# Value bias through spare contraction rows, and value blocks evacuated by ScalarE

## The chip, the cores and the metric

The kernel runs on one core of a Trainium2 chip. The metric is the device time of one launch in microseconds (us). The kernel before takes 1411.64 us (median of 3 runs, 1411.59 to 1412.21).

## The reference, cut to what matters

Input x has 16 batches of 512 tokens of width 128. Each batch is layer-normalised (xn), and the output is x plus an attention branch plus a feed-forward branch.

```python
q = einsum('bse,hde->bhsd', xn, Wq) + bq ; k = ... Wk + bk ; v = ... Wv + bv     # 16 heads of 64
scores = where(causal, -inf, q @ k.T / 8) ; att = softmax(scores) / 8
z = (att @ v).reshape(b, s, 1024) ; attention = z @ proj                          # 1024 x 128
base = xn @ W.T
lw = softmax(l2norm(xn @ Wp.T + bp) @ l2norm(sim) * exp(min(temp, c)))           # 4 experts
res = sum over experts of (lw if top1 else 0) * ((xn @ Wd.T) @ Wu.T)              # ranks 1, 2, 4, 8
out = x + attention + base + res
```

A row of softmax sums to 1, so the bias bv adds the same vector, bv / 8 carried through proj, to every token of the output. The attention weights are masked causally, and a softmax row still sums to 1 under the mask.

## The kernel before

**Units and steps.** A batch has 8 pairs of heads and 4 blocks of 128 queries, which makes 32 steps (`UNITS`). Step s handles pair s // 4 and block s % 4, whose scores are 128 x (128, 256, 384 or 512). Every engine walks the same list of steps, written out by hand in `step` functions, with semaphores between the engines. No planner reorders anything: the order of an engine's instructions is the order of the calls in its `step`.

**A unit's way.** TensorE (PE) writes the scores of both heads (L1046, L1049). VectorE (DVE) scales, masks and takes the maximum (`maximum`, L807). ScalarE (ACT) takes the exponentials with their sum (`exponentials`, L611). VectorE takes the reciprocal one step later (L796). GpSimd (POOL) multiplies by it (`normalise`, L534). TensorE transposes three steps after the scores (`LAG_T`, L1058), ScalarE copies head 0 out of PSUM (L622) and VectorE head 1 (L819). Once in four steps TensorE multiplies a pair by its values (`values`, L1082), nine steps after the pair began; ScalarE (L600) and VectorE (L825) split the result into a high and a low part, and `project` (L1094) multiplies that by proj. Four rotating buffers (`NROT`) hold the probabilities.

**Jobs.** `JOBS` lays other products over the steps, each in one of two PSUM banks (`jobp`, the step's parity): for each pair one q and one k product (L971), the router at step 5, the transposed xn of the next batch at step 25, the gated expert activations at step 26, and eight value blocks (128 tokens by 512 columns, L976) at steps 29, 30, 2, 6, 10, 14, 18 and 21. Steps 25 and 27 to 31 work ahead for the next batch. TensorE issues job s at the end of its step s, after `wait(pe, job_done[bank])` on the job before it in that bank. The other engines take up job s in their step s + 1. ScalarE does so early in the step, before its copy of the transposed probabilities (L622) and before its exponentials. VectorE does so late, after `maximum`, the reciprocal, L819 and L825. A value block is evacuated by VectorE alone in the kernel before: one `scalar_tensor_tensor` (L717) that multiplies by 1/8 and adds the bias, scaled once in the setup into `bv8` (L764). The bias reaches every partition by a broadcast DMA (L390).

**Other work around the change.** In step 21 VectorE gives the variances and GpSimd then normalises the next batch (`layernorm`, L490, L491, L496) before it goes on with the probabilities of unit 22. In step 22 TensorE transposes the finished sum into job bank 0 (L1119), and in step 23 VectorE adds the residual (`final`, L831). TensorE's k job of step 24 waits for that. In step 29 `lora` (L1108) adds the experts: one 96-row product of `wut` (up projections in three parts of 32 rows) with `gated_t` (the gated activations, same rows). SyncE issues all DMAs in order, among them the copies of q and k into `q_parts` and `k_twice` (L413, L417, L423), for which the next pair's scores wait.

**Setup.** GpSimd clears its tiles, makes the identity (L476) and the mask (L484) and normalises batch 0. TensorE transposes the weights. In batch 0, `rest` on TensorE (after step 0) transposes the small weights into `zp`, and `rest` on VectorE (after step 1) copies them out.

Of the kernel before, what the change touches and what calls it, by code (L numbers as in the profile page):

```python
# [34 lines left out]
F32 = mybir.dt.float32  # L35
F32R = mybir.dt.float32r
# [12 lines left out]
PROJ = 32  # L49
PARTS, PART = 3, NEXP * RMAX  # L50
NRD = PROJ + PART
LN_EPS = 1e-5
# [140 lines left out]
def build(nc, x, Wq, bq, Wk, bk, Wv, bv, proj, W, Wp, bp, sim, temp, Wd, Wu, out):  # L193
    with ExitStack() as ctx:
# [27 lines left out]
        up_parts = sb("up_parts", [P, PARTS, PART], F32R)  # L222
        wut = sb("wut", [PARTS * PART, E], F32R)
        bqk = sb("bqk", [P, 2 * NPAIR])
        bv8 = sb("bv8", [P, H * DH])
        bp_b = sb("bp_b", [P, PROJ])
# [46 lines left out]
        projs = pt[:, 1, 1, 0:2, :].rearrange("p a (c e) -> p (a c) e", e=E)  # L273
        bv_b = pt[:, 1, 1, 2:4, :].rearrange("p a b -> p (a b)")

# [14 lines left out]
        gated_parts = sb("gated_parts", [P, NBLK, PARTS, PART], F32R)  # L290
        gated_t = sb("gated_t", [PARTS * PART, S], F32R)

# [4 lines left out]
        proj_split = sem("proj_split")  # L297
        bv_loaded = sem("bv_loaded")
        sim_loaded = sem("sim_loaded")
        small_loaded = sem("small_loaded")  # L300
# [71 lines left out]
        def _(sp):  # L372
# [16 lines left out]
            load_weights(2, Wv)  # L389
            sp.dma_start(bv_b, bv.rearrange("h d -> (h d)").partition_broadcast(P)).then_inc(bv_loaded, 16)  # L390
            sp.wait_ge(zeroed, 8)
            sp.dma_start(small_in[:, 0, :], W).then_inc(small_loaded, 16)
            sp.dma_start(small_in[0:PROJ, 1, :], Wp).then_inc(small_loaded, 16)
# [69 lines left out]
        def _(pool):  # L463
# [6 lines left out]
            nc.gpsimd.memset(up_parts[:].bitcast(F32), 0.0).then_inc(zeroed, 1)  # L470
            nc.gpsimd.memset(small_in[:, 1:3, :], 0.0).then_inc(zeroed, 1)
            nc.gpsimd.memset(k_low[:].bitcast(F32), 0.0).then_inc(zeroed, 1)
            for e in range(NEXP):
                nc.gpsimd.memset(ramp[:, :, e:e + 1], float(NEXP - e)).then_inc(zeroed, 1)
            pool.wait_ge(zeroed, 8 + NEXP)
            nc.gpsimd.affine_select(out=ident[:], in_=ident[:], compare_op=ALU.not_equal, fill=1.0,  # L476
# [24 lines left out]
            layernorm(Counts(pool, -1))  # L501

            def pad_low_keys(c, s, setup=False):
# [4 lines left out]
                pool.wait_ge(zeroed, 8 + NEXP)  # L508
# [61 lines left out]
        def _(act):  # L570
# [7 lines left out]
            def job(c, s, back=0):  # L578
                kind, n = JOBS[s]
                bank = bank_of(s)  # L580
                if kind not in HI_KINDS:
                    return
                act.wait_ge(job_ready[bank], c.job(s, back))
                if kind == "xt":
                    nc.scalar.activation(xt_hi[:], jobp[bank][:], ACT.Copy)
                    nc.scalar.activation(by_parity(xq_hi[:]), evens_first(jobp[bank][:]), ACT.Copy)
                    nc.scalar.activation(xt[:], jobp[bank][:], ACT.Copy).then_inc(job_hi[bank], 1)
                elif kind == "k":
                    nc.scalar.activation(k_hi[:], jobp[bank][:], ACT.Identity,  # L589
                                         bias=bqk[:, NPAIR + n:NPAIR + n + 1]).then_inc(job_hi[bank], 1)  # L590
# [81 lines left out]
        def _(dve):  # L672
# [21 lines left out]
            def job(c, s, back=0):  # L694
                kind, n = JOBS[s]
                bank = bank_of(s)
                src = jobp[bank]
                if kind in HI_KINDS:

                    dve.wait_ge(job_hi[bank], c.hi(s, back))  # L700
                else:
                    dve.wait_ge(job_ready[bank], c.job(s, back))
# [8 lines left out]
                elif kind == "xt":  # L711
                    nc.vector.tensor_tensor(xt_lo[:], src[:], xt_hi[:].bitcast(F32), ALU.subtract)
                    done = nc.vector.tensor_tensor(by_parity(xq_lo[:]), evens_first(src[:]),  # L713
                                                   by_parity(xq_hi[:].bitcast(F32)), ALU.subtract)
                elif kind == "v":
                    cols = slice(S * (n // NBLK), S * (n // NBLK) + S)
# [39 lines left out]
            for s in AHEAD:  # L756
                job(before, s)
                if JOBS[s][0] == "xt":
                    weights(2)
                    dve.wait_ge(sim_loaded, 32)  # L760
                    nc.vector.tensor_scalar(temp_c[:], temp_b[:], CLAMP_MAX, None, ALU.min).then_inc(temp_ready, 1)
                if JOBS[s][0] == "k":
                    dve.wait_ge(bv_loaded, 16)
                    link(nc.vector.tensor_scalar(bv8[:], bv_b, INV_SCALE, None, ALU.mult))  # L764

# [11 lines left out]
            def rest():  # L777
# [5 lines left out]
                nc.vector.tensor_copy(wrd[:], zp[:, P:P + NRD]).then_inc(small_ready, 1)  # L783
                nc.vector.tensor_copy(wut[:], zp[0:PARTS * PART, 2 * P:3 * P]).then_inc(small_ready, 1)

# [152 lines left out]
            def batch(b, first, last):  # L938
                c = Counts(dve, b)
                for s in range(UNITS):  # L940
                    step(c, s, first, last)
                    if first and s == 1:
                        rest()

            batch(0, True, False)
# [9 lines left out]
        def _(pe):  # L955
# [192 lines left out]
            def batch(b, first, last):  # L1148
                c = Counts(pe, b)
                for s in range(UNITS):  # L1150
                    step(c, s, first, last)
                    if first and s == 0:
                        rest()

            batch(0, True, False)
# [30 lines left out]
```

## Time and profile before

| | |
|---|---|
| median of 3 runs | 1411.64 us |
| profiled execution | 1412.28 us |
| its span | 1410.0 us |
| granted TensorE clock, mean | 0.997 |
| busy: PE, PEld, DVE, ACT, POOL | 98%, 82%, 81%, 73%, 69% |

The profiled execution is 2.28 us longer than its span, which begins with the first instruction and ends with the last. PE is TensorE's matmul, PEld its weight load. A wait is the idle time of an engine in front of an instruction, put down to what released it. The ends of matmuls are modelled, so two neighbouring matmuls overlap in the rows, and distances between starts tell more than durations.

### The profile page before, as it was taken

What the parts mean: (1) busy time and instruction counts of PE and PEld (TensorE: products, weight loads), DVE (VectorE), ACT (ScalarE), POOL (GpSimd) and SP (SyncE); (2) the same over time, 40 slices, a digit from 0 to 9 for tenths busy, and PEclk for the clock granted to TensorE, in tenths of its full rate; (3) what the DMA queues carried; (4) which work ended last, traced back from release to release, by engine and by line L of the source; (5) the groups of instructions that cost most, each with busy time, mean ns of one, the idle gap of its engine ahead of it and who ended that gap; (6) DMA issues with size and microseconds to landing.
All of it is one profiled execution on the core that took longest, in us unless ns stands there. A gap on an engine that the chain in (4) does not pass through costs nothing. (4 is left out here: it accounts for less than half of the span.)

```text
span 1410.0 us, 34925 instructions
## 1 busy us (share of the span) xinstructions
PE 1378.1 (98%) x11036; PEld 1156.6 (82%) x11036; DVE 1141.5 (81%) x4134; ACT 1029.9 (73%) x3032; POOL 966.7 (69%) x1414
## 2 busy tenths in 40 slices
PE   6999999999999999999999999999999999999997
PEld 4778888788888888888888888888878888788886
DVE  6888878878788887977889788787878878888784
ACT  4777777777777776777777777777777777777774
POOL 5767767666676776767667676775776767677663
PEclk9999999999999999999999999999999999999999
DMA  6544444444454445444444544444444444444441
GB/s 154 117 102 103 116 112 94 110 116 102 106 116 115 94 106 123 95 115 100 113 109 109 121 95 106 113 113 106 103 110 112 98 117 110 113 100 112 106 98 46
DMA packets 113010, 151.91 MB, mean 108 GB/s; under 512 B 18175, under 2 KB 47166, under 8 KB 112830
## 3 DMA queue, kind: packets, MB, share of 16 engines
q1 hardware_dynamic: 112830, 149.68, 45.2%
q8 instruction: 92, 1.51, 0.5%
q14 instruction: 88, 0.72, 0.2%
HBM read 11.20 MB, written 4.19 MB: 11 GB/s over the span
## 5 line engine op out<-in xcount | busy, mean ns | idle before, releaser
L534 POOL TENSOR_TENSOR prob<-prob,rden 128x128 f32<-128x128 f32 (+3 forms) x1024 | 710.0, 720 | 383.4 <-DVE rden L796 381.1
L807 DVE CUSTOM_DVE_ANT_0 prob<-scores,mask 128x128 f32<-128x128 f32 (+3 forms) x1024 | 459.0, 484 | 233.1 <-issue 220.0
L611 ACT ACTIVATE prob<-prob,nmax 128x128 f32<-128x128 f32 (+3 forms) x1024 | 565.4, 556 | 69.1 <-DVE nmax L807 67.4
L1058 PE MATMUL ptp<-ident,prob 128*128 128x128 f32 x2560 | 370.5, 274 | 1.7 <-DVE pt L819 1.0
L622 ACT ACTIVATE pt<-ptp 128x128 f32<-128x128 f32 (+3 forms) x512 | 221.1, 432 | 170.3 <-PE ptp L1058 168.1
L1046 PE MATMUL scores<-k_twice,q_parts 128*128 128x128 f32 (+3 forms) x1024 | 328.4, 331 | 9.8 <-DMA k_twice<-k_hi 5.0
L1049 PE MATMUL scores<-k_low,q_parts 128*128 128x128 f32 (+3 forms) x1024 | 320.6, 323 | 0.0
L1058 PEld LDWEIGHTS ptp<-ident,prob 128*128 128x128 f32 x2560 | 295.4, 140 | 29.4 <-POOL prob L534 4.3
L1082 PE MATMUL zp<-pt,v_sb 128*64 128x64 f32 (+3 forms) x4096 | 307.7, 303 | 0.8 <-DVE z_lo L825 0.8
L1082 PEld LDWEIGHTS zp<-pt,v_sb 128*64 128x64 f32 x4096 | 221.5, 137 | 50.4 <-issue 22.3
L1046 PEld LDWEIGHTS scores<-k_twice,q_parts 128*128 128x128 f32 x1024 | 193.4, 189 | 67.8 <-issue 24.0
L819 DVE COPY pt<-ptp 128x128 f32<-128x128 f32 (+3 forms) x512 | 244.5, 478 | 4.3 <-PE ptp L1058 3.7
L1049 PEld LDWEIGHTS scores<-k_low,q_parts 128*128 128x128 f32 x1024 | 194.2, 190 | 19.2
L611 ACT ACTIVATION_READ_ACCUMULATOR prob<-prob,nmax 128x1 f32 x1024 | 197.1, 192 | 0.0
L513 POOL CAST k_low<-k_lo 64x512 fp32r<-64x512 f32 x256 | 155.9, 609 | 39.8 <-DVE k_lo L704 22.3
L600 ACT ACTIVATE z_hi<-zp 128x512 fp32r<-128x512 f32 x128 | 76.5, 598 | 120.5 <-PE zp L1082 119.4
L708 DVE SCALAR_TENSOR_TENSOR q_lo<-jobp,bqk,q_hi 128x512 fp32r<-128x512 f32 x128 | 94.7, 740 | 1.8 <-ACT q_hi L592 1.8
L704 DVE SCALAR_TENSOR_TENSOR k_lo<-jobp,bqk,k_hi 128x512 fp32r<-128x512 f32 x128 | 94.7, 740 | 0.0
L825 DVE TENSOR_TENSOR z_lo<-zp,z_hi 128x512 fp32r<-128x512 f32 x128 | 87.1, 681 | 3.2 <-ACT z_hi L600 3.2
L592 ACT ACTIVATE q_hi<-jobp,bqk 128x512 fp32r<-128x512 f32 x128 | 85.5, 668 | 4.6 <-PE jobp L971 4.6
L717 DVE SCALAR_TENSOR_TENSOR v_sb<-jobp,bv 128x512 f32<-128x512 f32 x128 | 87.0, 680 | 0.0
L589 ACT ACTIVATE k_hi<-jobp,bqk 128x512 fp32r<-128x512 f32 x128 | 86.3, 674 | 0.5 <-PE jobp L971 0.5
(141 smaller groups left out, 1689.7 us busy)
## 6 DMA issues: line engine op xcount, KB each, us to landing
k_twice<-k_hi SPq DMA_DIRECT2D x512, 128.0 KB, 2.4
q_parts<-q_hi SPq DMA_DIRECT2D x256, 128.0 KB, 2.4
q_parts<-q_lo SPq DMA_DIRECT2D x256, 128.0 KB, 2.4
xin<-in_L_attn_x_dram SPq DMA_DIRECT2D x16, 256.0 KB, 3.6
xres<-in_L_attn_x_dram SPq DMA_DIRECT2D x16, 256.0 KB, 3.1
out_dram<-osb SPq DMA_DIRECT2D x16, 256.0 KB, 2.5
pt<-in_L_attn_Wq_dram SPq DMA_DIRECT2D x1, 512.0 KB, 4.4
pt<-in_L_attn_Wk_dram SPq DMA_DIRECT2D x1, 512.0 KB, 4.8
```

The costliest lines, as they stand in the source:

```text
L513: nc.gpsimd.tensor_copy(k_low[own(h), h, n % 2, :], k_lo[own(h), :].bitcast(F32))\
L534: nc.gpsimd.tensor_tensor(part, part, scale, ALU.mult).then_inc(pn_ready, 1)
L611: nc.scalar.activation(part, part, ACT.Exp, bias=nmax[:, s % NROT, h:h + 1], scale=-1.0, accum_out=den[:, s % NROT, h:h + 1]).then_inc(p_r ...
L622: nc.scalar.activation(pt[:, p % 2, 0, 0:i + 1, P * i:P * i + P], src, ACT.Copy)\
L704: done = nc.vector.scalar_tensor_tensor(out=k_lo[:], in0=src[:], scalar=bqk[:, NPAIR + n:NPAIR + n + 1], in1=k_hi[:].bitcast(F32), op0=ALU ...
L708: done = nc.vector.scalar_tensor_tensor(out=q_lo[:, n % 2, :], in0=src[:], scalar=bqk[:, n:n + 1], in1=q_hi[:, n % 2, :].bitcast(F32), op0 ...
L807: nc.vector.tensor_tensor_reduce(out=prob[:, s % NROT, h, 0:cols], in0=scores[h][:, 0:cols], in1=mask[:, S - cols:S], scale=-INV_SCALE, sc ...
L819: nc.vector.tensor_copy(pt[:, p % 2, 1, 0:i + 1, P * i:P * i + P], src).then_inc(pt_ready[1], 1)
L1046: nc.tensor.matmul(scores[h][:, 0:width(s)], q_parts[:, h, p % 2, queries], k_twice[:, h, p % 2, 0:width(s)], start=True, stop=False)
L1049: nc.tensor.matmul(scores[h][:, 0:width(s)], q_parts[:, h, p % 2, queries], k_low[:, h, p % 2, 0:width(s)], start=False, stop=True).then_i ...
L1058: done = nc.tensor.transpose(ptp[h][:, P * j:P * j + P], prob[:, s % NROT, h, P * j:P * j + P], ident[:])
L1082: done = nc.tensor.matmul(zp[DH * odd:DH * odd + DH, z0 + P // 2 * j:z0 + S // 2], v_sb[:, j, col:col + DH], seen, start=j == NBLK - 1, st ...
```

## The change

Each value block is now evacuated by ScalarE as a copy scaled by 1/8, without a bias; VectorE does nothing for it. The bias enters through `lora`: `wut` and `gated_t` grow from 96 to 128 rows. The 32 added rows of `gated_t` hold zeros and ones that say which head a row of the kernel's reshaped output belongs to, 16 rows for the high and 16 for the low part. The added rows of `wut` hold bv / 8 carried through proj, one row for each head, in a high and a low part. They are made once: four small DMAs instead of the broadcast, three more memsets, three affine selects and one add on GpSimd, one more transpose in `rest`, eight matmuls after step 2 of batch 0 and two VectorE operations after step 3 of batch 0 (`value_bias`). The scaling of `bv8` goes from VectorE's setup, and a scaled copy `bvt` comes into its `rest`.

```diff
-            sp.dma_start(bv_b, bv.rearrange("h d -> (h d)").partition_broadcast(P)).then_inc(bv_loaded, 16)
             sp.wait_ge(zeroed, 8)
+            for part in range(2):
+                for odd in range(2):
+                    sp.dma_start(bv_rows[GATED + H * part:GATED + H * part + H, DH * odd:DH * odd + DH], bv)\
+                        .then_inc(bv_loaded, 16)
...
+            nc.gpsimd.memset(bv_rows, 0.0).then_inc(zeroed, 1)
             nc.gpsimd.memset(k_low[:].bitcast(F32), 0.0).then_inc(zeroed, 1)
+            nc.gpsimd.memset(token_heads, 1.0).then_inc(zeroed, 1)
+            nc.gpsimd.memset(late_rows[:], -1.0).then_inc(zeroed, 1)
...
+            rows_from(token_heads, 1, ROWS * GATED)
+            pool.wait_ge(heads_marked, 1)
+            rows_from(token_heads, -1, ROWS - 1 - ROWS * GATED)
+            nc.gpsimd.affine_select(out=late_rows[:], in_=late_rows[:], compare_op=ALU.is_ge, fill=0.0,
+                                    base=-(GATED + H), pattern=[[0, 1]], channel_multiplier=1).then_inc(heads_marked, 1)
+            pool.wait_ge(heads_marked, 2)
+            nc.gpsimd.tensor_tensor(gated_t[:], token_heads[:, 0:S], token_heads[:, S:2 * S], ALU.add)\
+                .then_inc(heads_marked, 1)
+            pool.wait_ge(heads_marked, 4)
...
# ScalarE, job
-                if kind not in HI_KINDS:
+                if kind not in HI_KINDS and kind != "v":
                     return
                 act.wait_ge(job_ready[bank], c.job(s, back))
+                if kind == "v":
+                    nc.scalar.activation(v_sb[:, n % NBLK, S * (n // NBLK):S * (n // NBLK) + S], jobp[bank][:], ACT.Copy,
+                                         scale=INV_SCALE).then_inc(job_done[bank], 1)
+                    return
...
# VectorE, job, setup and rest
+                if kind == "v":
+                    return
-                    done = nc.vector.scalar_tensor_tensor(
-                        out=v_sb[:, n % NBLK, cols], in0=src[:], scalar=INV_SCALE, in1=bv8[:, cols],
-                        op0=ALU.mult, op1=ALU.add)
-                    done = nc.vector.tensor_copy(gated_t[:], src[0:PARTS * PART, :])
+                    done = nc.vector.tensor_copy(gated_t[0:GATED, :], src[0:GATED, :])
-                    link(nc.vector.tensor_scalar(bv8[:], bv_b, INV_SCALE, None, ALU.mult))
+                nc.vector.tensor_scalar(bvt[:], zp[:, 3 * P:4 * P], INV_SCALE, None, ALU.mult).then_inc(small_ready, 1)
...
+            def value_bias():     # VectorE, after step 3 of batch 0
+                dve.wait_ge(bias_bank_ready, 1)
+                dve.wait_ge(heads_marked, 4)
+                link(nc.vector.tensor_copy(bias_hi[GATED:P, :], outp[GATED:P, 0:E]))
+                link(nc.vector.scalar_tensor_tensor(
+                    out=wut[GATED:P, :], in0=bias_hi[GATED:P, :].bitcast(F32), scalar=late_rows[GATED:P, 0:1],
+                    in1=outp[GATED:P, 0:E], op0=ALU.mult, op1=ALU.add))
...
# TensorE, rest
+                pe.wait_ge(bv_loaded, 64)
+                nc.tensor.transpose(zp[:, 3 * P:4 * P], bv_rows, ident[:])
+            def value_bias():     # TensorE, after step 2 of batch 0
+                pe.wait_ge(small_ready, 4)
+                pe.wait_ge(proj_loaded, 16)
+                for n in range(NPAIR):
+                    done = nc.tensor.matmul(outp[:, 0:E], bvt[:], projs[:, n, :], start=n == 0, stop=n == NPAIR - 1)
+                done.then_inc(bias_bank_ready, 1)
```

## Rows read from the trace of the kernel before

**Rows 1.** Waits, whole run: us in total, times, longest us

```profile
ACT pt L622 <- PE ptp L1058: 168.1, 211, 1.7
...
PEld jobp L971 <- DVE v_sb L717: 4.4, 20, 0.5
PEld ptp L1058 <- POOL prob L534: 4.3, 18, 0.7
```

**Rows 2.** Groups, ScalarE: a PSUM evacuation of a value block's size

```profile
L600 ACT ACTIVATE z_hi<-zp 128x512 fp32r<-128x512 f32 x128 | 76.5, 598 | 120.5 <-PE zp L1082 119.4
```

**Rows 3.** Timeline, TensorE, steps 0, 1, 4, 5: start, duration, operation

```profile
708.06 0.22 PE L1046 MATMUL scores<-k_twice,q_parts 128*128 128x128 f32 x1
...
709.85 0.27 PE L1046 MATMUL scores<-k_twice,q_parts 128*128 128x256 f32 x1
...
718.31 0.22 PE L1046 MATMUL scores<-k_twice,q_parts 128*128 128x128 f32 x1
...
719.86 0.28 PE L1046 MATMUL scores<-k_twice,q_parts 128*128 128x256 f32 x1
```

**Rows 4.** Timeline, VectorE and ScalarE, steps 31 and 0

```profile
794.03 0.68 DVE L717 SCALAR_TENSOR_TENSOR v_sb<-jobp,bv 128x512 f32<-128x512 f32 x1
...
792.47 0.28 ACT L622 ACTIVATE pt<-ptp 128x128 f32<-128x128 f32 x1 [0.37 <-PE ptp L1058]
```

**Rows 5.** Timeline, ScalarE, steps 3 and 22

```profile
717.00 0.28 ACT L622 ACTIVATE pt<-ptp 128x128 f32<-128x128 f32 x1 [0.37 <-PE ptp L1058]
...
767.25 0.60 ACT L622 ACTIVATE pt<-ptp 128x512 f32<-128x512 f32 x1 [1.42 <-PE ptp L1058]
```

**Rows 6.** Timeline, VectorE, steps 22 and 23

```profile
768.90 0.68 DVE L717 SCALAR_TENSOR_TENSOR v_sb<-jobp,bv 128x512 f32<-128x512 f32 x1
769.49 0.28 DVE L895 TENSOR_TENSOR gated<-dn,lg 128x128 f32<-128x128 f32 x1
...
771.41 0.68 DVE L831 TENSOR_TENSOR osb<-jobp,xres 128x512 f32<-128x512 f32 x1
```

**Rows 7.** Timeline, GpSimd, units 21 and 22 around the layer norm

```profile
767.92 1.19 POOL L534 TENSOR_TENSOR prob<-prob,rden 128x256 f32<-128x256 f32 x2 [0.84 <-DVE rden L796]
...
772.16 3.65 POOL L534 TENSOR_TENSOR prob<-prob,rden 128x384 f32<-128x384 f32 x4
```

**Rows 8.** Groups, GpSimd: one normalisation of 384 columns

```profile
L534 POOL TENSOR_TENSOR prob<-prob,rden 128x384 f32<-128x384 f32 x256 | 207.1, 830 | 187.8 <-DVE rden L796 187.8
```

**Rows 9.** Timeline, TensorE, k job of step 24; unit 22's second head in step 25

```profile
772.14 0.49 PE L971 MATMUL jobp<-xt_hi,w_hi 128*128 128x512 f32 x1
...
773.87 0.55 PE L1058 MATMUL ptp<-ident,prob 128*128 128x128 f32 x3
```

**Rows 10.** Timeline, GpSimd, setup

```profile
2.12 1.81 POOL L472 MEMSET k_low<- 128x2048 f32 x1
...
7.75 1.04 POOL L496 TENSOR_TENSOR xn<-xn,rstd 128x512 f32<-128x512 f32 x1
17.10 1.60 POOL L513 CAST k_low<-k_lo 64x512 fp32r<-64x512 f32 x2 [8.32 <-DVE k_lo L704]
```

**Rows 11.** Timeline, TensorE, setup and batch 0: steps 3, 5 and 8

```profile
9.62 1.06 PE L981 MATMUL jobp<-ident,xn 128*128 128x128 f32 x4
...
30.50 0.50 PE L1046 MATMUL scores<-k_twice,q_parts 128*128 128x512 f32 x1 [1.10 <-DVE nmax L807]
...
35.54 1.00 PE L986 MATMUL jobp<-wrd,xt 128*128 128x64 f32 x8
...
42.36 0.33 PE L1046 MATMUL scores<-k_twice,q_parts 128*128 128x128 f32 x1 [1.63 <-DMA k_twice<-k_hi]
```

**Rows 12.** Timeline, TensorE, batch 0: starts of steps 12 and 13

```profile
51.76 0.22 PE L1046 MATMUL scores<-k_twice,q_parts 128*128 128x128 f32 x1
...
53.91 0.39 PE L1046 MATMUL scores<-k_twice,q_parts 128*128 128x256 f32 x1
```

**Rows 13.** Windows: length, busy us and count of PE, PEld, DVE, ACT, POOL; granted clock; DMA

```profile
25.00:30.00 5.00, 4.19 (x14) 3.24 (x13) 3.54 (x15) 1.67 (x5) 1.98 (x4) 0.61 0.57 135
```

More of the change, by code:

```diff
@@ L50 @@
 PARTS, PART = 3, NEXP * RMAX
+GATED = PARTS * PART
 NRD = PROJ + PART
@@ L222, in build @@
         up_parts = sb("up_parts", [P, PARTS, PART], F32R)
-        wut = sb("wut", [PARTS * PART, E], F32R)
+        wut = sb("wut", [P, E], F32R)
+        bvt = sb("bvt", [P, P])
+        late_rows = sb("late_rows", [P, 1])
+        bias_hi = sb("bias_hi", [P, E], F32R)
         bqk = sb("bqk", [P, 2 * NPAIR])
-        bv8 = sb("bv8", [P, H * DH])
         bp_b = sb("bp_b", [P, PROJ])
@@ L273, in build @@
         projs = pt[:, 1, 1, 0:2, :].rearrange("p a (c e) -> p (a c) e", e=E)
-        bv_b = pt[:, 1, 1, 2:4, :].rearrange("p a b -> p (a b)")
+        bv_rows = pt[:, 1, 1, 2, 0:P]
+        token_heads = pt[:, 1, 0, 2:4, :].rearrange("p a b -> p (a b)")
         z_hi = sb("z_hi", [P, 2, NPAIR, OCT, ROWS], F32R)
@@ L290, in build @@
         gated_parts = sb("gated_parts", [P, NBLK, PARTS, PART], F32R)
-        gated_t = sb("gated_t", [PARTS * PART, S], F32R)
+        gated_t = sb("gated_t", [P, S], F32R)
         w_loaded = [sem(f"w_loaded{n}") for n in range(3)]
@@ L298, in build @@
         bv_loaded = sem("bv_loaded")
+        heads_marked = sem("heads_marked")
+        bias_bank_ready = sem("bias_bank_ready")
         sim_loaded = sem("sim_loaded")
@@ L471, in _ @@
             nc.gpsimd.memset(small_in[:, 1:3, :], 0.0).then_inc(zeroed, 1)
+            nc.gpsimd.memset(bv_rows, 0.0).then_inc(zeroed, 1)
             nc.gpsimd.memset(k_low[:].bitcast(F32), 0.0).then_inc(zeroed, 1)
+            nc.gpsimd.memset(token_heads, 1.0).then_inc(zeroed, 1)
+            nc.gpsimd.memset(late_rows[:], -1.0).then_inc(zeroed, 1)
             for e in range(NEXP):
                 nc.gpsimd.memset(ramp[:, :, e:e + 1], float(NEXP - e)).then_inc(zeroed, 1)
-            pool.wait_ge(zeroed, 8 + NEXP)
+            pool.wait_ge(zeroed, 11 + NEXP)
             nc.gpsimd.affine_select(out=ident[:], in_=ident[:], compare_op=ALU.not_equal, fill=1.0,
@@ L501, in _, with rows_from @@
             layernorm(Counts(pool, -1))
+            def rows_from(tile, step, base):
+                nc.gpsimd.affine_select(out=tile, in_=tile, compare_op=ALU.is_ge, fill=0.0, base=base,
+                                        pattern=[[step, tile.shape[1]]], channel_multiplier=-ROWS * step)\
+                    .then_inc(heads_marked, 1)
[6 more added lines that the diff above has]
+            nc.gpsimd.tensor_tensor(gated_t[:], token_heads[:, 0:S], token_heads[:, S:2 * S], ALU.add)\
+                .then_inc(heads_marked, 1)
+            pool.wait_ge(heads_marked, 4)
             def pad_low_keys(c, s, setup=False):
@@ L507, in pad_low_keys @@
                 scaled = 0 if setup else c.fixed(c.head(s, 1))
-                pool.wait_ge(zeroed, 8 + NEXP)
+                pool.wait_ge(zeroed, 11 + NEXP)
                 if not setup:
@@ L714, in job @@
                                                    by_parity(xq_hi[:].bitcast(F32)), ALU.subtract)
-                elif kind == "v":
-                    cols = slice(S * (n // NBLK), S * (n // NBLK) + S)
-                    done = nc.vector.scalar_tensor_tensor(
-                        out=v_sb[:, n % NBLK, cols], in0=src[:], scalar=INV_SCALE, in1=bv8[:, cols],
-                        op0=ALU.mult, op1=ALU.add)
                 elif kind == "router":
@@ L761, in _ @@
                     nc.vector.tensor_scalar(temp_c[:], temp_b[:], CLAMP_MAX, None, ALU.min).then_inc(temp_ready, 1)
-                if JOBS[s][0] == "k":
-                    dve.wait_ge(bv_loaded, 16)
-                    link(nc.vector.tensor_scalar(bv8[:], bv_b, INV_SCALE, None, ALU.mult))
             dve.wait_ge(small_loaded, 16 * n_small)
@@ L783, in rest @@
                 nc.vector.tensor_copy(wrd[:], zp[:, P:P + NRD]).then_inc(small_ready, 1)
-                nc.vector.tensor_copy(wut[:], zp[0:PARTS * PART, 2 * P:3 * P]).then_inc(small_ready, 1)
+                nc.vector.tensor_copy(wut[0:GATED, :], zp[0:GATED, 2 * P:3 * P]).then_inc(small_ready, 1)
+                nc.vector.tensor_scalar(bvt[:], zp[:, 3 * P:4 * P], INV_SCALE, None, ALU.mult).then_inc(small_ready, 1)
                 dve.wait_ge(simnorm_ready, 1)
@@ L943, in batch @@
                         rest()
+                    if first and s == 3:
+                        value_bias()
             batch(0, True, False)
@@ L1153, in batch @@
                         rest()
+                    if first and s == 2:
+                        value_bias()
             batch(0, True, False)
```

## The prediction

> **What bounds the kernel now.** The table of busy time comes first: TensorE is busy for 98% of the span, VectorE 81%, ScalarE 73%. The list of waits comes next, for what TensorE still waits for. Its weight loads stop 20 times for VectorE's copy of a value block, 4.4 us in all, and 18 times for GpSimd, 4.3 us; ScalarE stands 168.1 us waiting for TensorE's transposes [rows 1]. So TensorE's own order sets the end. The change takes no instruction from it, and can shorten the time only where TensorE stands. The timelines show where that is in a batch of some 88 us (1410 / 16): at the k jobs of steps 0 and 24, at the transposes of step 25 and around step 27. In between its starts follow one another at an even pace.
>
> **The steady part: what VectorE loses.** It sheds 8 operations of 0.68 us per batch [rows 4], 87 us in 16 batches. What this is worth is read at each place where TensorE waits.
>
> *Step 0.* The k job needs bank 0, which the value block of step 30 leaves when VectorE has copied it at 794.03 + 0.68 [rows 4]. Step 0 lasts 709.85 - 708.06 = 1.79 us; step 4, with the same instructions, 719.86 - 718.31 = 1.55 us [rows 3]. The difference, 0.24 us, is the wait and what it costs just after. ScalarE takes the same block in its step 31, before the copy in front of which it stands 0.37 us idle, at 792.47 [rows 4]. The value block's product is over by then, so ScalarE's copy ends near 792.8, two microseconds before TensorE needs the bank. The wait goes in 15 batches: 15 x 0.24 = 3.6 us. Nothing is late next: VectorE also loses the copy of the block of step 29, which stands in front of its maximum for unit 31, so that maxima, exponentials and the q copies of the pair come earlier as well.
>
> *Steps 23 to 25.* VectorE's value copy at 768.90 pushes what follows to 769.49, and with it `final`, which ends at 771.41 + 0.68 = 772.09 [rows 6]; TensorE's k job starts at 772.14, just behind [rows 9]. Without the copy, `final` ends some 0.59 us earlier (769.49 - 768.90), and so do the maxima of step 23. TensorE would arrive at step 25 that much sooner. But there it needs unit 22 from GpSimd, and GpSimd's order is fixed by something else: unit 21 at 767.92, as soon as VectorE's reciprocal of step 22 releases it, then the layer norm, then unit 22 from 772.16 [rows 7]. Two normalisations of 0.83 us [rows 8] end at 773.82, and TensorE's second head starts at 773.87 [rows 9]. That chain starts in front of the removed copy and has none of it in it. The 0.59 us are handed back in step 25: I count 0 here. The other end is the whole of it, 15 x 0.59 = 8.9 us.
>
> *Steps 27 and 28.* No value block lies between step 21 and this place, and the copies of steps 29 and 30 come after it: 0.
>
> **What ScalarE gains.** A copy of 128 x 512 out of PSUM takes it 598 ns [rows 2]; the scale is part of the instruction and there is no bias operand. 8 x 16 of them are 77 us more. In step 22 it lies in an idle 1.42 us; in steps 3, 7, 11, 15 and 19 the idle is only 0.37 us [rows 5], so 0.23 us stick out and push the exponentials of that step, the q and k copies and their DMAs. The units concerned are normalised far ahead of their transposes three steps later; the only place where TensorE regularly waits for GpSimd is step 25 (18 waits in 16 batches [rows 1]). I count 0; the other end is a rival below.
>
> The Trainium skill speaks against the move: "ScalarE: Activation LUTs", Rules for kernel authors, gives multiplications to VectorE and budgets about 0.3 us plus 0.83 ns per element on ScalarE, an estimated 0.73 us for this copy. The row has 0.598 us for the same shape against 0.68 us on VectorE, so the measurement decides against the rule here; by its price 0.36 us instead of 0.23 us would stick out.
>
> **`lora`.** 128 rows instead of 96 stream the same 512 columns. The nearest row is a 128-row product of 512 columns, 0.49 us [rows 9]. If rows cost time, a quarter of it would be the 32 new ones: at most 0.12 x 16 = 2.0 us, at least 0. I take 0, since the weight load is hidden beside the product in front of it and the stream of columns is unchanged.
>
> **Setup.** On GpSimd a memset of 2048 columns takes 1.81 us [rows 10], so 128 + 1024 + 1 more columns ahead of the identity are about 1.1 us. The layer norm ended at 8.79 (7.75 + 1.04 [rows 10]) and now ends near 9.9; TensorE took it up at 9.62 [rows 11]. Cost 0.3 us. The selects and the add that follow (some 4 us, scaled from the layer norm's 1.04 us for 512 columns) lie in the 8.32 us that GpSimd waits before 17.10 [rows 10]; 0, and if that cover were too short, the excess. The broadcast DMA goes and four short ones come on SyncE, ahead of loads that are needed only after step 0: 0. VectorE's scaling of `bv8` goes off no path, and the operation on `bvt` takes about 0.3 us in front of a maximum for which TensorE waits.
>
> **Batch 0.** One more transpose, 0.2 us. The eight matmuls: the router's four products are eight instructions within 1.00 us, about 0.1 us each at 64 columns [rows 11]; at 128 columns I take 0.11 us, and 16 x 0.11 = 1.8 us. TensorE stood 1.10 us before step 3 anyway [rows 11], so 0.7 us are new. Together 0.3 + 0.2 + 0.7 = 1.2 us, and 0.1 us for ScalarE's value copy in step 3. The wait of 1.63 us for k_twice before step 8 [rows 11] does not absorb them, since the q and k jobs of steps 3 and 4 that feed these DMAs move too. VectorE's two operations of about 0.3 us take the place of the value copy of step 2. Against this, batch 0 has no `project`, so TensorE is faster and runs into VectorE: step 12 lasts 53.91 - 51.76 = 2.15 us [rows 12] against 1.55 us later, 0.60 us of waits behind a value copy, and steps 16 and 20 are like it: 3 x 0.60 = 1.8 us that go. What goes at steps 23 and 24 is handed back in step 25 as above. Batch 0: 1.3 - 1.8 = -0.5 us.
>
> **The sum.** -3.6 - 0.5 = -4.1 us. The profiled execution took 1412.28 us (2.28 us more than its span) and would take 1408.2; the median of the runs lies 0.64 us lower, so 1407.5 us. The likeliest case has its own range: 1409.3 without the gain of batch 0, 1405.7 if setup and value bias cost only 0.2 us (1.1 less) and the later waits for k_twice shrink by 0.05 us in each batch.
>
> **Rivals.**
>
> *A. GpSimd does not hand the 0.59 us back.* Its chain from 767.92 would have to be shorter without VectorE working beside it. For it: GpSimd's wait at that place is released by VectorE. Against it: that release comes before the removed copy, and the distance from 772.16 to 773.82 is made of GpSimd's own durations. 1407.5 - 8.9 = 1398.6 us. 12%.
>
> *B. The start costs more.* TensorE's clock was granted at 0.61 between 25 and 30 us [rows 13], that is at half (1.2 GHz) for part of it, after an idle stretch. If the eight matmuls ran at half, 1.8 us more; if the gain of batch 0 fails too, another 1.8 us: 1411.1 us. 14%. "TensorE: Matmul & The Clock Gate" of the Trainium skill, Part 1, says that half clock is the default state and activity lifts it; by that rule the matmuls themselves would help to end it, and the row of 30 us and later would be the one to follow.
>
> *C. Slower: ScalarE becomes late.* Place: steps 3, 7, 11, 15 and 19. If TensorE stood for what sticks out, 5 x 0.23 x 16 = 18.4 us: 1425.9 us. It decides once the units behind have less than 0.23 us in hand before their transposes. For it: ScalarE goes from 73% to 79% and works in order, so a value copy blocks exponentials. Against it: the 18 waits for GpSimd, one per batch and all explained by the layer norm. 8%.
>
> *D. The change does not do what it says.* The wait at step 0 stays because TensorE finds another one there, the maximum of unit 31 or a DMA: 1407.5 + 3.6 = 1411.1 us. 6%.
>
> **How the numbers follow.** Forecast 60%, A 12%, B 14%, C 8%, D 6%. A run of this kernel can tell a difference of about 0.2%, 2.8 us, so faster means below 1408.8 us. Faster: 0.51 of the forecast's 0.60, and A's 0.12: 0.63. Same: the remaining 0.09, B and D: 0.29. Slower: C, 0.08. The range reaches from 1401.0, which holds a partial A, to 1412.5, which holds B and D with a us to spare; all of A and C, 20%, may lie outside.
>
> **What would show it.** Right: no wait of the k job for v_sb; step 0 lasts 1.55 us; `final` ends about 3.6 us after GpSimd starts on unit 21 instead of 4.17 (772.09 - 767.92), while unit 22's second head is transposed 5.95 us after GpSimd starts on unit 21 (773.87 - 767.92) as before; step 8 of batch 0 starts 1 to 1.5 us later and step 21 about 0.5 us sooner than in the trace of before. Wrong: step 25 no longer waits for GpSimd (A), TensorE waits for ScalarE's pt or for GpSimd in other steps (C), or a step 0 of 1.79 us (D).

## The result, and the profile after

The changed kernel takes 1407.54 us (median of 7 runs, 1405.42 to 1408.1), the kernel before 1412.21 us on the same chip (median of 7, 1411.08 to 1414.11). The ratio is 0.9965, with a 95% interval of 0.9953 to 0.9976. The forecast was 1407.5 us.

The profiled execution took 1408.1 us (span 1406.4, mean granted clock 0.997), against 1412.28 us (span 1410.0). The page after, its busy times:

```profile
PE 1371.4 (98%) x11053; PEld 1161.0 (83%) x11053; DVE 1093.6 (78%) x4008; ACT 1085.1 (77%) x3160; POOL 970.6 (69%) x1421
```

VectorE went from 81% to 78% and ScalarE from 73% to 77%. These are averages, and say nothing yet about the time. The list of waits (whole run: us in total, times, longest) answers [rows 1]:

```profile
ACT pt L654 <- PE ptp L1106: 102.0, 116, 1.6
...
ACT v_sb L613 <- PE jobp L1014: 13.2, 32, 1.1
...
PE ptp L1106 <- DVE pt L855: 7.2, 16, 0.8
...
PEld jobp L1009 <- DVE osb L867: 5.0, 15, 0.3
...
PEld ptp L1106 <- POOL prob L562: 4.4, 18, 0.7
```

TensorE no longer waits for v_sb. ScalarE lost 66 us of its idle time in front of L654 (168.1 in [rows 1]), which is where most of the 75 us of new copies went. The 18 waits for GpSimd are as before (15 of them in step 25, one for each batch but the last, and three in the tail of the last batch; the prediction put all 18 down to the layer norm), and so are the 15 for `final` (L867; before 5.0 us for L831). New are 16 waits of TensorE for VectorE's copy of transposed probabilities (L855), 7.2 us in all; in the kernel before that row has 1.0 us in 2 waits.

**Step 0.** TensorE's timeline (start, duration), steps 0 and 1, beside [rows 3]:

```profile
705.62 0.22 PE L1094 MATMUL scores<-k_twice,q_parts 128*128 128x128 f32 x1
...
707.16 0.28 PE L1094 MATMUL scores<-k_twice,q_parts 128*128 128x256 f32 x1
```

707.16 - 705.62 = 1.54 us; batches 1 to 15 have 1.55 to the rounding. It was 1.79. Batch 0 is another case, below.

**Steps 22 to 24.** First VectorE beside [rows 6], then GpSimd beside [rows 7], then TensorE beside [rows 9]:

```profile
765.92 0.68 DVE L861 TENSOR_TENSOR z_lo<-zp,z_hi 128x512 fp32r<-128x512 f32 x1
766.52 0.35 DVE L931 TENSOR_TENSOR gated<-dn,lg 128x128 f32<-128x128 f32 x1
...
768.02 0.89 DVE L937 CAST gated_parts<-gated 128x256 fp32r<-128x256 f32 x1
768.83 0.15 DVE L832 RECIPROCAL rden<-den 128x2 f32<-128x2 f32 x1
768.91 0.26 DVE L855 COPY pt<-ptp 128x128 f32<-128x128 f32 x1
769.09 0.67 DVE L867 TENSOR_TENSOR osb<-jobp,xres 128x512 f32<-128x512 f32 x1
```

```profile
765.54 1.18 POOL L562 TENSOR_TENSOR prob<-prob,rden 128x256 f32<-128x256 f32 x2 [0.89 <-DVE rden L832]
766.68 1.06 POOL L502 TENSOR_TENSOR rstd<-var_eps,power 128x4 f32<-128x4 f32 x1
767.72 1.04 POOL L503 TENSOR_TENSOR xn<-xin,meanvar 128x512 f32<-128x512 f32 x1
768.84 1.04 POOL L508 TENSOR_TENSOR xn<-xn,rstd 128x512 f32<-128x512 f32 x1
769.84 4.37 POOL L562 TENSOR_TENSOR prob<-prob,rden 128x384 f32<-128x384 f32 x6
```

```profile
768.49 0.41 PE L1106 MATMUL ptp<-ident,prob 128*128 128x128 f32 x2
769.31 0.41 PE L1106 MATMUL ptp<-ident,prob 128*128 128x128 f32 x2 [0.42 <-DVE pt L855]
769.82 0.50 PE L1009 MATMUL jobp<-xt_hi,w_hi 128*128 128x512 f32 x1
```

The value copy is gone: L931 follows 0.60 us behind the start of L861, where it used to follow 1.19 us behind (769.49 - 768.30). But `final` ends at 769.09 + 0.67 = 769.76, which is 4.22 us after GpSimd starts on unit 21 (765.54). Before it was 4.17. The 0.59 us are already lost inside VectorE, before TensorE can see them. One row shows where: the cast L937 takes 0.89 us. Before, the same instruction (L901) in the same place took 0.32 us:

```profile
770.91 0.32 DVE L901 CAST gated_parts<-gated 128x256 fp32r<-128x256 f32 x1
```

Both casts end 0.15 us after GpSimd's subtraction `xn<-xin,meanvar` ends: before 771.23 against 770.04 + 1.04 = 771.08 (L491), after 768.91 against 767.72 + 1.04 = 768.76 (L503). The cast came earlier by the whole removed copy, and waited until the same instruction of GpSimd was over. TensorE then stands in step 24 in front of L1106 and in front of the k job.

**Balance of the span.** From the starts of the batches: batch 1 starts 0.19 us later, batches 1 to 14 together 3.18 us shorter (14 times 0.24 is 3.36), and the last batch with the tail 0.67 us shorter. The sum is 3.66 us, the difference of the spans (1410.03 and 1406.37). An undisturbed batch went from 85.72 to 85.79 us down to 85.60. That is 0.12 to 0.19 us, the 0.24 us of step 0 less 0.06 in steps 23 to 25 (2.69 + 2.41 + 4.15 before, 2.62 + 2.54 + 4.15 now). The rest of the 3.18 us is that five of the 14 batches of before lasted over 86 us, four of them through a k_twice transfer that came late before step 4 and one (batch 2) through longer steps 16 and 24, and only one does now. The medians differ by 4.67 us, more than the spans, because the time outside the span fell as well: it is 1.70 to 1.92 us in the seven runs of the changed kernel and 2.28 us in the profiled execution of the kernel before. No term of the forecast had these 0.4 us.

### The profile page after: what moved, and what is told of

Same layout as the page of the kernel before. It is cut to its first block, busy times and chain, and to the rows that moved or that the text cites. A ratio compares the mean times of both kernels' runs of the same rounds, so it can differ in the third digit from the quotient of the medians.

```text
span 1406.4 us, 34974 instructions
## 1 busy us (share of the span) xinstructions
PE 1371.4 (98%) x11053; PEld 1161.0 (83%) x11053; DVE 1093.6 (78%) x4008; ACT 1085.1 (77%) x3160; POOL 970.6 (69%) x1421
## 4 chain that ended last, share of the span: by engine, by line
PE 52%; DVE 3%; issue 1%; ACT 1%; SPq 0%; DMA 0%; DVEq 0%
PE zp L1130 12%; PE ptp L1106 11%; PE jobp L1009 7%; PE scores L1094 7%; PE scores L1097 6%; PE jobp L1014 4%; PE outp L1142 3%; DVE prob L843 1%; PE jobp L1024 1%; DVE osb L867 0%; DVE gated_parts L937 0%; DVE xq_lo L747 0%; PE jobp L1019 0%; PE jobp L1167 0%; PE outp L1156 0%
## 5 line engine op out<-in xcount | busy, mean ns | idle before, releaser
L843 DVE CUSTOM_DVE_ANT_0 prob<-scores,mask 128x128 f32<-128x128 f32 (+3 forms) x1024 | 461.0, 486 | 276.1 <-issue 253.3
L1106 PE MATMUL ptp<-ident,prob 128*128 128x128 f32 x2560 | 372.1, 274 | 8.0 <-DVE pt L855 7.2
L1106 PEld LDWEIGHTS ptp<-ident,prob 128*128 128x128 f32 x2560 | 295.4, 141 | 37.5 <-issue 11.1
L654 ACT ACTIVATE pt<-ptp 128x128 f32<-128x128 f32 (+3 forms) x512 | 221.4, 432 | 104.0 <-PE ptp L1106 102.0
L855 DVE COPY pt<-ptp 128x128 f32<-128x128 f32 (+3 forms) x512 | 246.0, 480 | 4.3 <-PE ptp L1106 3.7
L861 DVE TENSOR_TENSOR z_lo<-zp,z_hi 128x512 fp32r<-128x512 f32 x128 | 87.1, 680 | 3.2 <-ACT z_hi L632 3.2
L613 ACT ACTIVATE v_sb<-jobp 128x512 f32<-128x512 f32 x128 | 75.0, 586 | 13.3 <-PE jobp L1014 13.2
```

The lines of the kernel that those rows point to most:

```text
L654: nc.scalar.activation(pt[:, p % 2, 0, 0:i + 1, P * i:P * i + P], src, ACT.Copy)\
L843: nc.vector.tensor_tensor_reduce(out=prob[:, s % NROT, h, 0:cols], in0=scores[h][:, 0:cols], in1=mask[:, S - cols:S], scale=-INV_SCALE, sc ...
L855: nc.vector.tensor_copy(pt[:, p % 2, 1, 0:i + 1, P * i:P * i + P], src).then_inc(pt_ready[1], 1)
L1106: done = nc.tensor.transpose(ptp[h][:, P * j:P * j + P], prob[:, s % NROT, h, P * j:P * j + P], ident[:])
```

## The experiments

Each kernel was timed beside the kernel before (1412.6 us in both sets), with 11 runs each, but 6 of the kernel without the value bias and 4 of the changed kernel with the layer norm split. Two theories stand at first. **Pinned:** GpSimd's layer norm holds both `final` (through the cast) and unit 22, so only step 0 gains. **Rival:** something that the change added (the start, ScalarE's copies) eats a gain that steps 23 to 25 would have had.

**No value bias.** It leaves the value bias out of the output, so that the price of the start shows.

```diff
-                nc.tensor.matmul(outp[:], wut[:], gated_t[:], start=False, stop=False, skip_group_check=True)
+                nc.tensor.matmul(outp[:], wut[0:GATED, :], gated_t[0:GATED, :], start=False, stop=False, skip_group_check=True)
...
-                    if first and s == 2:
-                        value_bias()
```

Its DMAs, memsets, selects, add, transpose and `bvt` go as well.

> The changed kernel without everything that makes the bias (four small DMAs, three memsets, the selects and the add on GpSimd, the transpose, the eight matmuls, the VectorE operations; lora with 96 rows), so bv is left out of the output. ScalarE still evacuates the value blocks. The theory that the start pays for the bias (1.0 us at step 8 of batch 0 in the trace of after): step 8 of batch 0 starts at 42.3 instead of 43.36 us, and the time is 1406.5, 1.0 us below the changed kernel. Rival, that the waits of batch 0 absorb the bias work: step 21 of batch 0 starts at 73.8 as before and the time is 1407.5.

1407.69 us (1405.88 to 1409.6), ratio 0.9968 [0.9957, 0.998]. In the trace step 8 of batch 0 starts at 42.30 instead of 43.36 us and batch 1 at 105.15 instead of 106.16: the bias costs 1.0 us, once, inside the span (the granted clock between 25 and 30 us is alike in the two traces, 0.55 and 0.59). The time is not 1.0 us lower, against the theory: outside the span these runs spend 2.08 to 2.17 us, some 0.3 us more than the changed kernel, and the runs do not resolve the rest. The steps of the steady part are the same, so the 128-row `lora` costs nothing that can be seen.

**Copies back on VectorE.** The bias stays in the spare rows, the value blocks go back to VectorE as scaled copies.

```diff
-                if kind == "v":
-                    return
...
+                elif kind == "v":
+                    done = nc.vector.tensor_scalar(v_sb[:, n % NBLK, S * (n // NBLK):S * (n // NBLK) + S], src[:],
+                                                   INV_SCALE, None, ALU.mult)
```

> The changed kernel with the value blocks evacuated by VectorE again, as a scaled copy without the bias operand; the bias stays in the spare rows. The theory that the gain is the k job's wait at step 0 and nothing of the bias path: a copy of about 0.68 us on VectorE brings back steps 0 of 1.79 us (15 x 0.24 = 3.6 us) and the waits of batch 0, with the price of the start on top: 1412 to 1413 us. Rival, that one operand less in VectorE's evacuation (or the bias path) already gave the gain: 1407.5 to 1409 us.

1412.26 us (1411.07 to 1414.17), ratio 1.0002 [0.9994, 1.0011]. Step 0 is 1.78 us again. So, within the 1.2 us that the interval leaves, the whole gain comes from the engine that copies, not from where the bias enters.

**Cast behind `final`.** Of the changed kernel: the cast that waits for GpSimd is issued later in step 23.

```diff
-                    router(c, 2 * s)
+                    if s != STEP_FINAL:
+                        router(c, 2 * s)
...
+                if s == STEP_FINAL:
+                    router(c, 2 * s)
                 router(c, 2 * s + 1)
```

> The changed kernel with one VectorE instruction moved within step 23: the cast of gated_parts, which ran 0.89 us instead of 0.32 us beside GpSimd's layer norm, is issued after final instead of ahead of the reciprocal. Theory A, that the cast waits for GpSimd's instruction to end and that unit 22's normalisation on GpSimd holds the same 0.59 us a second time: final ends 0.8 us sooner, the k job of step 24 no longer waits for it, the second head of unit 22 is still transposed 5.95 us after GpSimd starts on unit 21 or only as much earlier as the reciprocal of unit 22 moves, and the time stays within 2 us of 1407.5. Theory B, that the cast alone held the gain back: step 24 loses its 0.6 us and step 25 does not win them, 15 x 0.6 = 9 us less, 1398.5 us. In both the cast takes about 0.3 us plus whatever is left of GpSimd's instruction at its new place.

1414.21 us (1412.54 to 1417.71), ratio 1.0011 [1.0001, 1.0021]: slower than either theory had it. VectorE's timeline, then two rows of GpSimd's:

```profile
769.24 0.68 DVE L867 TENSOR_TENSOR osb<-jobp,xres 128x512 f32<-128x512 f32 x1
769.84 1.15 DVE L937 CAST gated_parts<-gated 128x256 fp32r<-128x256 f32 x1
771.02 0.80 DVE L941 TENSOR_TENSOR gated_parts<-gated,gated_parts 128x128 fp32r<-128x128 f32 x1
```

```profile
769.80 1.04 POOL L508 TENSOR_TENSOR xn<-xn,rstd 128x512 f32<-128x512 f32 x1
770.80 4.42 POOL L562 TENSOR_TENSOR prob<-prob,rden 128x384 f32<-128x384 f32 x6
```

`final` did come earlier: 769.92, which is 3.42 us after unit 21 begins at 766.50. But the cast now met the next instruction of the layer norm, L508, from its start, and again ended 0.15 us after it (770.99 and 770.84). L941, with two inputs in SBUF, then met the first normalisation. The maxima of step 24 came late behind both, and TensorE stood 1.14 us before step 25; an undisturbed batch takes 86.02 us, 0.4 us more than in the changed kernel. Delaying an instruction by some tenths only changes which GpSimd instruction it waits for.

This trace also warns of something else. Up to step 22 its batch 0 has the instructions of the changed kernel, and yet step 8 begins at 40.61 us instead of 43.36 and batch 1 at 103.62 instead of 106.16. The granted clock is 1.00 between 20 and 30 us here, and 0.72 and 0.59 in the two halves of that stretch in the changed kernel. So a difference of a microsecond or two in batch 0 between two single traces is not by itself the price of an edit.

**Layer norm split.** Of the changed kernel: GpSimd takes only the root in step 21 and does the subtraction and the multiplication after unit 22, so VectorE and TensorE no longer meet them there.

```diff
-            def layernorm(c):
+            def root(c):
...
+            def layernorm(c):
...
                     if s == STEP_VAR and not last:
+                        root(c)
+                    if s == STEP_VAR + 1 and not last:
                         layernorm(c)
```

`root` keeps the power (L502 of the changed kernel), `layernorm` the two others (L503, L508).

> The changed kernel with GpSimd's layer norm split: the root stays in step 21, the subtraction and the multiplication come after unit 22's normalisation instead of before it. Both things that pin steps 23 to 25 go: the cast finds GpSimd idle (0.29 us instead of 0.89), unit 22 is normalised as soon as its reciprocal is there. Theory A expects the waits for pt in step 24 and for GpSimd in step 25 gone (0.59 and 0.19 us) and the wait for final at 0 to 0.34 us: 0.7 to 1.1 us in each of 15 batches, 1391 to 1397 us. Rival, that TensorE then waits for unit 23, which GpSimd normalises later (3.06 and 2.50 us in hand now), or for the late xn in step 25: 1405 us or more.

1398.7 us (1396.03 to 1399.73), ratio 0.9902 [0.9886, 0.9917]: the fastest kernel of the study, 0.6% below the changed one, and 1.7 us above what theory A expected. VectorE, GpSimd and TensorE at the same place:

```profile
764.09 0.28 DVE L941 CAST gated_parts<-gated 128x256 fp32r<-128x256 f32 x1
764.29 0.15 DVE L836 RECIPROCAL rden<-den 128x2 f32<-128x2 f32 x1
764.37 0.26 DVE L859 COPY pt<-ptp 128x128 f32<-128x128 f32 x1
764.56 0.67 DVE L871 TENSOR_TENSOR osb<-jobp,xres 128x512 f32<-128x512 f32 x1
```

```profile
761.61 1.18 POOL L564 TENSOR_TENSOR prob<-prob,rden 128x256 f32<-128x256 f32 x2 [0.88 <-DVE rden L836]
762.76 1.06 POOL L501 TENSOR_TENSOR rstd<-var_eps,power 128x4 f32<-128x4 f32 x1
764.52 1.66 POOL L564 TENSOR_TENSOR prob<-prob,rden 128x384 f32<-128x384 f32 x2 [0.71 <-DVE rden L836]
766.15 1.04 POOL L504 TENSOR_TENSOR xn<-xin,meanvar 128x512 f32<-128x512 f32 x1
```

```profile
764.56 0.63 PE L1110 MATMUL ptp<-ident,prob 128*128 128x128 f32 x4
765.28 0.50 PE L1013 MATMUL jobp<-xt_hi,w_hi 128*128 128x512 f32 x1
...
766.57 0.82 PE L1110 MATMUL ptp<-ident,prob 128*128 128x128 f32 x6
```

With GpSimd idle the cast takes 0.28 us. `final` ends at 765.23, 3.62 us after unit 21 starts. The transposes of step 24 run without a break, and so do those of step 25. Step 24 lasts 1.94 us (2.54 in the changed kernel), step 25 3.96 (4.15), and a batch 84.83 us instead of 85.6. Of TensorE's waits around here only 0.34 us for `final` is left. These 0.78 us per batch are what was expected (0.7 to 1.1). What is missing lies in batch 0, where TensorE's clock was at its lower level, 1.2 GHz, twice. The windows below have length, busy us and count of PE, PEld, DVE, ACT, POOL, then clock, DMA share, GB/s. Between 25 and 30 us the clock is 0.50, and the first 1.5 us of the sixteen bias matmuls fall into it (each of the eight calls is two instructions in the trace): they take 2.67 us instead of 1.96. Step 8 still begins at 43.23 us, 0.13 sooner than in the changed kernel. The larger loss follows: TensorE stands 1.71 us for k_twice before step 8, the clock falls soon after (0.50 in a window from 43.77 to 47.18 us), and steps 8 to 11 take 11.02 us instead of 9.43. In the changed kernel the wait at that place is 1.58 us and the clock stays at 1.00. Batch 1 starts 0.77 us later for all this.

```profile
25.00:30.00 5.00, 4.79 (x18) 4.19 (x17) 4.47 (x20) 1.52 (x5) 1.99 (x4) 0.50 0.55 132
...
45.00:50.00 5.00, 5.00 (x45) 4.05 (x43) 3.06 (x9) 2.69 (x10) 4.59 (x8) 0.78 0.62 144
```

```profile
28.61 2.67 PE L1085 MATMUL outp<-pt,bvt 128*128 128x128 f32 x16
```

**No cast.** It leaves the cast out (a four-column memset keeps its semaphore), so the experts' high parts are stale. The question: if the cast alone is removed and the layer norm stays, is there a gain?

```diff
-                    nc.vector.tensor_copy(gated_parts[:, :, 0:PARTS:2, :],
-                                          gated[:].unsqueeze(2).to_broadcast([P, NBLK, 2, PART])).then_inc(r_chain, 1)
+                    nc.vector.memset(scratch[:], 0.0).then_inc(r_chain, 1)
```

> The changed kernel without the cast of gated_parts (a memset of 4 columns stands in its place, so the experts' high parts are stale in the output). VectorE then meets no port held by GpSimd ahead of final; GpSimd's order is untouched. Theory A, that unit 22's place behind the layer norm on GpSimd pins step 25 by itself: final ends about 3.6 us after GpSimd starts on unit 21 (4.22 in the changed kernel), step 24 shrinks from 2.54 to about 2.0 us, and step 25 grows by as much, so the second head of unit 22 is still transposed 5.95 us after that start: 1407.5 us within 1. Theory B, that the cast's wait alone held the gain: step 25 keeps its 4.15 us, 15 x 0.55 = 8 us less, 1399 us.

1410.08 us (1407.99 to 1412.58), ratio 0.9983 [0.9974, 0.9991]. No gain, though the cast is gone and `final` ends 3.42 us after unit 21 starts. Steps 24 and 25 last 2.19 and 4.49 us, in sum 6.68; with the cast 2.54 and 4.15, in sum 6.69. The 0.35 us won in step 24 return in step 25, where TensorE still waits for unit 22 and also for a maximum that stands behind the next VectorE operation, L941, which now meets GpSimd in place of the cast. Of the two waits the one for unit 22 ends last: its second head starts 6.00 us after GpSimd starts on unit 21, as with the cast (6.01). The rows are VectorE's, GpSimd's and TensorE's:

```profile
770.63 0.68 DVE L868 TENSOR_TENSOR osb<-jobp,xres 128x512 f32<-128x512 f32 x1
771.23 1.14 DVE L941 TENSOR_TENSOR gated_parts<-gated,gated_parts 128x128 fp32r<-128x128 f32 x1
```

```profile
771.18 1.04 POOL L509 TENSOR_TENSOR xn<-xn,rstd 128x512 f32<-128x512 f32 x1
```

```profile
772.63 0.39 PE L1094 MATMUL scores<-k_twice,q_parts 128*128 128x256 f32 x1 [0.30 <-DVE nmax L844]
...
773.89 0.55 PE L1106 MATMUL ptp<-ident,prob 128*128 128x128 f32 x3 [0.19 <-POOL prob L563]
```

L941 ends at 772.37, 0.15 us after L509 (772.22). A batch lasts 85.77 us, 0.17 more than in the changed kernel: the rest of its steps are up to 0.03 us longer each, for a reason that was not found, and 15 times that is the 2.5 us between the two medians, which neither theory had.

**The kernel before with the layer norm split.** The same edit as above, applied to the kernel before.

> The kernel before with GpSimd's layer norm split in the same way, value copies on VectorE. The theory that the split only uncovers what the moved value copy is worth: here VectorE's value copy still delays the maxima of step 23 and final (0.80 us of waits in steps 23 and 24), only the wait of 0.19 us in step 25 goes: 15 x 0.19 = 2.8 us, 1409.5 us. The moved copies are then worth 1409.5 - 1398.7 = 10.8 us on top of the split and 4.7 us without it. Rival, that the split alone gives its 8.9 us in any kernel: 1403 us.

1409.98 us (1406.99 to 1412.09), ratio 0.9979 [0.9969, 0.9988]. A batch takes 85.55 us, step 25 3.97, but step 24 still 2.38 and step 0 1.79. Side by side, in us:

| layer norm | copies on VectorE | copies on ScalarE | the move is worth |
|---|---|---|---|
| in one piece | 1412.2 | 1407.5 | 4.7 |
| split | 1410.0 | 1398.7 | 11.3 |

The times come from different sets of runs and are good to about 1.5 us each. The undisturbed batches say the same without that noise: 85.77 and 85.60 us in one piece, 85.55 and 84.83 us split. The two edits are not additive: each uncovers what the other was hidden behind.

**Only the block of step 30 on ScalarE.** Of the changed kernel; the other seven go back to VectorE.

```diff
-                if kind == "v":
+                if s == 30:
                     return
...
+                elif kind == "v":
+                    done = nc.vector.tensor_scalar(v_sb[:, n % NBLK, S * (n // NBLK):S * (n // NBLK) + S], src[:],
+                                                   INV_SCALE, None, ALU.mult)
```

> The changed kernel with only the value block of step 30 evacuated by ScalarE, the other seven by VectorE as scaled copies. If the steady gain is the k job's wait at step 0 alone: steps 0 of 1.55 us, all other steps as with VectorE's copies, 15 x 0.24 = 3.6 us under the kernel with all copies on VectorE (1412.3): 1408.7 us. If it is spread over the eight blocks: 1/8 of it, 1411.7 us or more.

1411.03 us (1409.24 to 1412.2), ratio 0.9988 [0.9979, 0.9997], 2.3 us above what was expected. In the trace step 0 lasts 1.55 us and steps 23 and 24 are 2.69 and 2.42, as with all copies on VectorE. So one block of eight brings the whole steady gain: its undisturbed batches take 85.55 us, no more than the changed kernel's 85.6. In the time, though, it brings only 1.2 of the 4.7 us (1412.26 - 1411.03). What is missing lies outside the undisturbed batches. Its span is 3.1 us longer than the changed kernel's: 0.66 us up to the start of batch 1 (steps 12 and 20 stay long at 2.12 and 2.02, and the bias matmuls take 2.62 us, the first 1.4 us of them at a granted clock of 0.50), 0.5 us in the last batch and tail (step 24 is 2.39 there), and 1.9 us in between, where more batches have a late k_twice transfer. Why more of them were late here was not found.

**Every value block copied twice by ScalarE.** The price of ScalarE's load, doubled.

```diff
                 if kind == "v":
+                    nc.scalar.activation(scratch[:, n % 2, :], jobp[bank][:], ACT.Copy, scale=INV_SCALE)
```

> The changed kernel with each value block copied twice by ScalarE (the first copy into a spare tile), 0.6 us more in eight steps, 77 us of ScalarE in all. If the units behind have slack (0.7 us and more in hand in every step but 25): about 0.85 us stick out in steps 3, 7, 11, 15 and 19 and TensorE still does not stand for most of it: 1408 to 1411 us. If ScalarE is at the edge after the change: each doubled copy costs its length where it sticks out, 5 x 0.6 x 16 = 48 us, 1455 us.

1410.24 us (1408.56 to 1412.96), ratio 0.9987 [0.9978, 0.9996]. ScalarE's groups (us in total, mean ns, idle before):

```profile
L614 ACT ACTIVATE scratch<-jobp 128x512 f32<-128x512 f32 x128 | 75.0, 586 | 13.3 <-PE jobp L1016 13.3
L615 ACT ACTIVATE v_sb<-jobp 128x512 f32<-128x512 f32 x128 | 75.9, 593 | 0.0
```

75 us more on ScalarE leave every steady step as it was (85.60 us for a batch). What is lost is in batch 0, which is 0.87 us longer, most of it in steps 13, 17 and 21, and in batches with a late transfer. There TensorE stands 0.19 us for ScalarE's pt in step 13 and its weight load 0.37 us for GpSimd in step 21, waits that the changed kernel's batch 0 does not have. So rival C's kind of cost is there at twice the load, but only in batch 0.

## Why the prediction was right, and where it was not

**Step 0: right.** 1.79 became 1.55 us in every batch from batch 1 on. It is the whole steady gain, and the block of step 30 alone brings it.

**Steps 23 to 25: net right, the path to it wrong.** The prediction said that `final` "ends some 0.59 us earlier" and that the 0.59 us "are handed back in step 25". `final` ended no earlier (4.22 us after unit 21 starts instead of 3.6), and steps 24 and 25 last 2.54 and 4.15 us: it was handed back one step earlier, in step 24. The failed step is the sum on VectorE: it took the distance from the value copy to `final` as VectorE's own durations, 2.51 us, which would only slide. One of them, the cast, was not its own: it ended with an instruction of GpSimd. [Rows 6] leave that row out: its 0.32 us looked like a plain duration, and only the comparison with GpSimd's timeline gives it away (the cast ends 0.15 us after L491). The rule stands in the Trainium skill, "SBUF — State Buffer", SBUF: two separate sides: a VectorE operation in a two-port mode, or with two inputs in SBUF (this only against a GpSimd operation that reads SBUF, as those here do), shares a port pair with the GpSimd operation, and the later one is held until the earlier one's whole instruction is over. The traces agree, with 0.89, 1.15 and 0.28 us for one and the same cast. The pin that the prediction did name is real as well: the weight load of unit 22's second head starts 6.01 us after unit 21 does (5.95 forecast, rows below), and in the kernel without the cast it starts 6.00 us after, so this pin takes the gain back without the cast's help.

TensorE's weight loads in the changed kernel:

```profile
771.55 0.31 PEld L1106 LDWEIGHTS ptp<-ident,prob 128*128 128x128 f32 x3 [0.20 <-POOL prob L562]
```

The last batch has no layer norm on GpSimd. There the cast takes 0.28 us and step 24 went from 2.40 to 1.92 us, a gain of 0.48 us that the forecast did not have, and that the pinned theory explains.

**Rival A** (GpSimd does not hand it back, 1398.6 us): refuted for this change. The 1398.7 us of the kernel with the layer norm moved are close to its number by luck: its terms were 15 x 0.59 = 8.9 us, and the steady gain there is 0.78 us in each batch, less what batch 0 lost at the lower clock.

**ScalarE: right.** The copy takes 586 ns (598 taken), and the units behind it have more in hand than it costs. Rival C fails even at twice the load: no steady step grows, and the time rises by 2.7 us where it had 18.4 us at the single load. The copy is faster on ScalarE than the 0.68 us on VectorE.

**`lora`: right** at 0 us.

**Start: right in size.** Step 0 begins at 22.61 us, 0.25 later (0.3 said), and step 8 1.0 us later (1 to 1.5 said). The sixteen bias matmuls take 1.96 us (1.8 said) from 29.59 on; the granted clock is 0.59 between 25 and 30 us, but 1.00 in a window from 29.06 us on, so all of them ran at 2.4 GHz. In this kernel rival B did not come. In the one with the split layer norm it did, for 0.7 us on the same matmuls and 1.6 us in steps 8 to 11, and in the one with only the block of step 30 on ScalarE for 0.66 us on the matmuls.

**Batch 0: mis-sized.** 1.8 us were to go at steps 12, 16 and 20. Step 12 went from 2.15 to 1.70 and step 20 from 2.03 to 1.65, but step 16 only from 2.17 to 1.95, where the maximum is late by itself, and the step before step 20 grew by 0.13. About 0.95 us went, so step 21 starts at 73.81 and not 0.5 us before 73.76; up to batch 1 the change costs 0.19 us instead of gaining 0.5. Against it stand the last batch, 0.43 us better than forecast, the fewer late transfers and the 0.4 us outside the span, which no step of the forecast had. The errors nearly cancel: part of the exactness of 1407.5 is luck.

## What to carry to other kernels

Before shifting a VectorE instruction between two SBUF tiles (a cast, a copy, a product of two SBUF tiles), lay its end beside GpSimd's timeline: if it ends just behind a GpSimd instruction, part of its duration may be a wait, and then it will not slide with the work in front of it. Where an engine's relief brings less than its path says, look for the second instruction that pins the same place; here moving GpSimd's layer norm by one unit turned a gain of 4.7 us into 13.9 (1412.6 - 1398.7). And price a moved load at each place where the bound engine waits: of eight copies moved, one brought the whole gain of an undisturbed batch, though not the gain of the first and the last batch.

## What the runs showed of the hardware

The same cast of 128 x 256 took 0.28, 0.32, 0.89 and 1.15 us, according to how much of GpSimd's instruction was left when it was issued, and ended 0.15 us after that instruction each time it was held. The products of two SBUF tiles did the same: in the kernel without the cast L941 ended 0.15 us after L509, and in the changed kernel L931 took 0.35 us instead of 0.28 and ended 0.15 us after GpSimd's normalisation of unit 21 (766.87 and 766.72). The maxima (L843), which read PSUM and one SBUF tile, and `final` kept their 0.68 and 0.67 us beside the same instructions. The group of the layer norm's root, a GpSimd instruction of four columns, has 1.01 us in the kernels with the copies on VectorE (before, copies back on VectorE, one block on ScalarE, before with the split) and 1.05 to 1.06 us in the others; it lies in the chain that ends at unit 22 and is the 0.06 us that steps 23 to 25 lost. The long ones are those of the kernels in which L931, just before, was held; no run isolates whether that is the cause.
